# A gated FFN kernel: other order of SyncE's first loads, narrower first products of zeros, biases transposed behind q's product

## Chip, cores, metric

One Trainium2 chip, one core. The metric is the device time of one execution in microseconds (us). TensorE is called PE here, VectorE DVE, ScalarE ACT, GpSimd POOL, SyncE SP.

## What is computed

x has 128 batches of 32 rows of 256 (f32). With q = relu(cond · W3 + b3), one row of 256 for each batch, the reference does

```
c   = relu(((32 * x + sum of x over the 32 rows) * q) @ W2 + b2)
h1  = c @ w1q.T ;  h3 = c @ w3q.T          # hidden size 682
out = x + (silu(h1) * h3) @ w2q.T
wq  = clip(round(w / s), -1, 1) * s,  s = mean(|w|)   # for w1, w3, w2
```

## The kernel before, in words

The 4096 rows of x are eight groups of 512 rows, and each group is two halves of 256 rows. Half n goes through these steps: a product that brings it into transposed form, a scaling by q, a product with W2 (`project_c`), relu, and a split of the result into a high and a low part (`c_hi`, `c_lo`). A group then goes through six hidden steps (five blocks of 128 hidden units and a rest of 42): two products of four passes each, silu, product, split, and the output product. From about 21 us on, PE is nearly always busy with this loop.

The change is in the start, before that loop. Here the four engines run lists that are written out by hand, and semaphores tie them together:

- SP issues the loads in order: two bias loads of two rows each (`b_rows`, semaphore `got_b`), half 0 of x (`load_half(0)`), W2 (`got_W2`), halves 1 and 2 of x, then w1, w3, half 3, w2 and the other groups. ACT issues the loads of cond (`got_cond`) and W3 (`got_W3`) at the same time.
- DVE clears `blank`, a bf16 tile of zeros, then builds `mix`, the 128x128 matrix that both multiplies x by 32 and adds the sum over the sequence.
- PE multiplies zeros by zeros `WARM_UP` times (L422, nothing reads the results), transposes cond (L425), transposes the four bias rows into four columns (L427), does one more product of zeros (L428), and makes q's product in two chunks (L432, four recorded passes). ACT copies the transposed cond (L255) ahead of q's product, and DVE copies the bias columns (L605).
- ACT turns q's product into `qT` (L259). It needs the bias columns for that. DVE's first scaling waits for `qT`.
- `mix_x(n)` on PE (L377) is the transposing product of half n, eight recorded passes. DVE's `scale_mixed(n)` (L545) scales the result by q. `project_c(n)` (L391), eight recorded passes, needs the scaled half and W2. ACT's relu (L269) follows.
- ACT sums |w1| and |w3| (L278), PE adds these sums over the partitions (`sum_partitions`, L397), DVE makes a limit from each (L575) and compares the weights with it (L581). The compared weights are transposed on PE (L403) and their signs are taken on ACT (L284, L288). The first hidden products (L461) need them.

PE's order in the start is: products of zeros, cond, biases, zeros, q, `mix_x(0)`, `mix_x(1)`, `project_c(0)`, `mix_x(2)`, `project_c(1)`, `sum_partitions(0)`, `project_c(2)`, `sum_partitions(1)`, and then transposed weights and `mix_x(3)`.

Of the kernel before, what the change touches and what calls it, by code (L numbers as in the profile page):

```python
# [7 lines left out]
BF16 = mybir.dt.bfloat16  # L8
# [2 lines left out]
AX = mybir.AxisListType  # L11

P = 128
WARM_UP = 5
BANK = 512


def adaln_ternary_ffn_kernel(nc, x, cond, W3, b3, W2, b2, w1, w3, w2, out):
# [3 lines left out]
    DC = D // P  # L22
# [24 lines left out]
    with ExitStack() as ctx:  # L47
        def sb(name, shape, dt):
            return ctx.enter_context(nc.sbuf_tensor(name, shape, dt))

        def sem(name):
            return ctx.enter_context(nc.semaphore(name))

        cond_sb = sb("cond_sb", [P, Q], F32)
        b_rows = sb("b_rows", [2 * DC, P], F32)
# [22 lines left out]
        ident = sb("ident", [P, P], F32)  # L78
# [1 line left out]
        ones = sb("ones", [P, P], F32)  # L80

        mix = sb("mix", [P, P], F32)
        blank = sb("blank", [P, BANK], BF16)
        warm = sb("warm", [P, 1], F32)

        xo = sb("xo", [P, NG, TT, D], F32)
# [15 lines left out]
        bank = ctx.enter_context(nc.psum_tensor("bank", [P, 8, BANK], F32))  # L102
# [8 lines left out]
        b_cols_ps = bank[:, 3, 0:2 * DC]  # L111
# [13 lines left out]
        got_cond, got_W3, got_W2, got_b = sem("got_cond"), sem("got_W3"), sem("got_W2"), sem("got_b")  # L125
# [8 lines left out]
        b_cols_done, b_cols_copied = sem("b_cols_done"), sem("b_cols_copied")  # L134
# [39 lines left out]
        @block.sync  # L174
        def _(sp):
            for free in o_free:
                sp.sem_inc(free, 1)
            def load_half(n):
                g, h = n // HALVES, n % HALVES
                sp.dma_start(xo[:, g, h * HTT:(h + 1) * HTT], x_v[g, :, h * HTT:(h + 1) * HTT]).then_inc(got_half[n], 16)  # L180

            sp.dma_start(b_rows[0:DC, :], b3.rearrange("(c p) -> c p", p=P)).then_inc(got_b, 16)
            sp.dma_start(b_rows[DC:2 * DC, :], b2.rearrange("(c p) -> c p", p=P)).then_inc(got_b, 16)
            load_half(0)
            sp.dma_start(W2_sb[:], W2.rearrange("(c p) n -> p c n", p=P)).then_inc(got_W2, 16)
            load_half(1)
            load_half(2)

            sp.wait_ge(zeroed, 2)
            sp.dma_start(w1_sb[:, 0:HC, :], w1[0:HC * P, :].rearrange("(j p) d -> p j d", p=P)).then_inc(got_w1, 16)  # L190
            sp.dma_start(w1_sb[0:HR, HC, :], w1[HC * P:H, :]).then_inc(got_w1, 16)
            sp.dma_start(w3_sb[:, 0:HC, :], w3[0:HC * P, :].rearrange("(j p) d -> p j d", p=P)).then_inc(got_w3, 16)
            sp.dma_start(w3_sb[0:HR, HC, :], w3[HC * P:H, :]).then_inc(got_w3, 16)
            load_half(3)
            sp.dma_start(w2_sb[:], w2.rearrange("(c p) h -> p c h", p=P)).then_inc(got_w2, 16)
            for g in range(AHEAD, NG):
                if g == NG - 3:

                    sp.wait_ge(ternary_done, 5)
                sp.dma_start(xo[:, g], x_v[g]).then_inc(got_group[g - AHEAD], 16)  # L200
            for g in range(NG - 1):
                for b in range(TT // 2):
                    sp.wait_ge(o_free[b], g + 2)
                    sp.dma_start(out_v[g, :, 2 * b:2 * b + 2], xo[:, g, 2 * b:2 * b + 2]).then_inc(stored, 16)
            for b, t0, t1, n in ((0, 0, 2, 1), (1, 2, 3, 1), (1, 3, 4, 2)):
                sp.wait_ge(o_free[b], NG + n)
                sp.dma_start(out_v[NG - 1, :, t0:t1], xo[:, NG - 1, t0:t1]).then_inc(stored, 16)
            sp.wait_ge(stored, 16 * (NG * (TT // 2) + 1))
# [141 lines left out]
        def _(pe):  # L350
# [18 lines left out]
            def mix_x(n):  # L369

                pe.wait_ge(got_half[n], 16)
                bank_of_x_free(n)
                xT = xT_of(n)
                for c in range(DC):
                    for t in range(HTT):
                        col = c * HT + t * P
                        last = pe.matmul(xT[:, col:col + P],  # L377
                                         xo[:, n // HALVES, n % HALVES * HTT + t, c * P:(c + 1) * P], mix[:],
                                         start=True, stop=True)
                last.then_inc(xT_done, 1)  # L380
# [38 lines left out]

            pe.wait_ge(blank_ready, 1)  # L420
            for _ in range(WARM_UP):
                pe.matmul(bank[:, 7, :], blank[:, 0:P], blank[:], start=True, stop=True)  # L422
            pe.wait_ge(const_ready, 2)
            pe.wait_ge(got_cond, 16)
            pe.transpose(condT_ps, cond_sb[:], ident[:]).then_inc(condT_done, 1)  # L425
            pe.wait_ge(got_b, 16 * 2)
            pe.transpose(b_cols_ps, b_rows[:], ident[0:2 * DC, 0:2 * DC]).then_inc(b_cols_done, 1)  # L427
            pe.matmul(bank[:, 7, :], blank[:, 0:P], blank[:], start=True, stop=True)  # L428
            pe.wait_ge(got_W3, 16)
            pe.wait_ge(condT_copied, 1)  # L430
            for c in range(DC):
                pe.matmul(qT_ps[:, c, :], W3_sb[:, c * P:(c + 1) * P], condT[:], start=True, stop=True  # L432
                          ).then_inc(q_done, 1)
            pe.wait_ge(mix_ready, 6)
            mix_x(0)
            mix_x(1)
# [265 lines left out]
```

## Time and profile before

| | |
|---|---|
| median of 3 runs | 176.47 us (176.46 to 176.51) |
| profiled execution, its own time | 176.39 us |
| its span, first to last instruction | 174.2 us (so 2.2 us lie around it) |
| mean granted TensorE clock | 0.998 |
| PE busy | 169.4 us, 97% of the span |
| DVE, ACT, POOL busy | 59%, 50%, 20% |
| moved by DMA | 11.11 MB |

All times below are counted from the start of the span. In a row of the timeline the first number is the start, the second the time from the start of the first instruction to the end of the last of a merged group, and "x" the number of instructions in it. Passes of PE overlap, so a merged group tells more about the pace than the duration of one pass does. Brackets tell how long the engine was idle before and what ended that.

### The profile page before, as it was taken

The numbers are of one execution on the slowest core, as the hardware profiler recorded it, in microseconds if no ns is written. First come the engines' busy times: TensorE is split into PE (matmuls) and PEld (weight loads), VectorE is DVE, ScalarE is ACT, GpSimd is POOL, SyncE is SP. The second block draws the span as 40 slices with busy tenths as digits, with TensorE's granted clock in tenths as the row PEclk, the third lists the DMA queues.
The fourth block names the chain that finished last, engine by engine and source line by source line (L and its number), as shares of the span: only waits on it lengthen the run. The fifth ranks groups of instructions, "written<-read, shape, count | busy, mean of one in ns | idle before, by whom it ended". The sixth has DMA issues, their size and how long they took to land.

```text
span 174.2 us, 2563 instructions
## 1 busy us (share of the span) xinstructions
PE 169.4 (97%) x966; PEld 145.4 (83%) x966; DVE 103.1 (59%) x170; ACT 87.0 (50%) x161; POOL 34.6 (20%) x38
## 2 busy tenths in 40 slices
PE   7999999999999999999999999999999999999993
PEld 2988777888888888888889888888889888988792
DVE  2339939654864279353874369443874439456763
ACT  4169873645543372555534282554535285254640
POOL 5000005710505050320605041230605020000000
PEclk9999999999999999999999999999999999999999
DMA  4999082000030003000030003000030003000303
GB/s 141 311 360 349 32 268 93 0 4 4 0 120 0 4 0 120 0 0 4 0 120 0 0 4 109 11 0 0 4 120 0 0 4 120 4 0 0 120 4 120
DMA packets 10901, 11.11 MB, mean 64 GB/s; under 512 B 561, under 2 KB 10633, under 8 KB 10889
## 3 DMA queue, kind: packets, MB, share of 16 engines
q1 hardware_dynamic: 10600, 10.75, 18.8%
q10 hardware_dynamic: 288, 0.20, 0.4%
q8 instruction: 8, 0.13, 0.3%
q14 instruction: 5, 0.03, 0.1%
HBM read 6.75 MB, written 4.19 MB: 63 GB/s over the span
## 4 chain that ended last, share of the span: by engine, by line
PE 90%; DVE 3%; DMA 2%; SPq 1%; ACT 1%; POOL 1%; issue 0%; POOLq 0%; ACTq 0%
PE bank L461 46%; PE bank L490 24%; PE bank L391 15%; PE bank L365 3%; DMA xo<-in_x_dram 2%; DVE w_t L581 2%; PE bank L377 1%; POOL x L228 1%; PE bank L415 0%; DVE x L545 0%; DVE vsum L550 0%; DVE y L557 0%; ACT silu L323 0%; ACT T L284 0%; DVE xo L648 0%
## 5 line engine op out<-in xcount | busy, mean ns | idle before, releaser
L461 PE MATMUL bank<-c_hi,T 128*128 128x512 f32 (+1 forms) x176 | 71.1, 404 | 0.2 <-ACT T L288 0.2
L461 PE MATMUL bank<-c_lo,T 128*128 128x512 f32 (+1 forms) x176 | 69.5, 395 | 0.0
L323 ACT ACTIVATE silu<-bank,checked 128x512 f32<-128x512 f32 (+1 forms) x48 | 33.0, 688 | 72.1 <-PE bank L461 72.1
L635 DVE TENSOR_TENSOR gf<-silu,bank 128x512 f32<-128x512 f32 (+1 forms) x48 | 32.9, 685 | 53.4 <-PE bank L461 44.7
L461 PEld LDWEIGHTS bank<-c_hi,T 128*128 128x128 f32 (+1 forms) x176 | 32.8, 186 | 6.8 <-ACT T L288 0.6
L461 PEld LDWEIGHTS bank<-c_lo,T 128*128 128x128 f32 (+1 forms) x176 | 32.8, 187 | 6.2
L490 PE MATMUL bank<-T,g_hi 128*128 128x256 f32 x160 | 34.1, 291 | 0.0
L233 POOL TENSOR_TENSOR c_lo<-ct,c_hi 128x512 fp32r<-128x512 f32 x12 | 17.6, 1470 | 82.1 <-ACT c_hi L274 82.1
L490 PE MATMUL bank<-T,g_lo 128*128 128x256 f32 x160 | 32.6, 281 | 0.0
L391 PE MATMUL bank<-x,W_sb 128*128 128x256 f32 x128 | 30.5, 381 | 0.5 <-POOL x L228 0.4
L642 DVE TENSOR_TENSOR g_lo<-gf,g_hi 128x512 fp32r<-128x512 f32 x40 | 29.0, 724 | 1.2 <-ACT g_hi L330 1.2
L490 PEld LDWEIGHTS bank<-T,g_hi 128*128 128x128 f32 x160 | 26.5, 188 | 2.0
L391 PEld LDWEIGHTS bank<-x,W_sb 128*128 128x128 f32 x128 | 23.5, 190 | 4.0 <-POOL x L228 0.6
L490 PEld LDWEIGHTS bank<-T,g_lo 128*128 128x128 f32 x160 | 24.9, 188 | 0.0
L330 ACT CAST g_hi<-gf 128x512 fp32r<-128x512 f32 x40 | 24.5, 611 | 0.0
L228 POOL TENSOR_TENSOR x<-y,qT 128x512 f32<-128x512 f32 x12 | 12.6, 1050 | 23.3 <-DVE y L557 23.3
L269 ACT ACTIVATE ct<-bank,b_cols 128x256 f32<-128x256 f32 x32 | 13.3, 471 | 3.8 <-PE bank L391 3.8
L648 DVE SCALAR_TENSOR_TENSOR xo<-bank,out_scale,xo 128x512 f32<-128x512 f32 (+1 forms) x17 | 11.4, 709 | 1.4 <-PE bank L490 1.3
L550 DVE TENSOR_REDUCE vsum<-bank 128x16 f32<-128x512 f32 x12 | 8.2, 681 | 2.9 <-PE bank L365 2.9
L557 DVE SCALAR_TENSOR_TENSOR y<-bank,vsum 128x512 f32<-128x512 f32 x12 | 8.2, 685 | 0.2
L274 ACT CAST c_hi<-ct 128x512 fp32r<-128x512 f32 x12 | 7.6, 631 | 0.0
L365 PE MATMUL bank<-ident,xo 128*128 128x128 f32 x48 | 7.2, 273 | 0.0
(61 smaller groups left out, 82.4 us busy)
## 6 DMA issues: line engine op xcount, KB each, us to landing
out_dram<-xo SPq DMA_DIRECT2D x15, 256.0 KB, 2.2
xo<-in_x_dram SPq DMA_DIRECT2D x6, 512.0 KB, 7.3
w_sb<-in_L_ffn_w_dram SPq DMA_DIRECT2D x2, 640.0 KB
xo<-in_x_dram SPq DMA_DIRECT2D x4, 256.0 KB, 4.8
w_sb<-in_L_ffn_w_dram SPq DMA_DIRECT2D x1, 682.0 KB, 8.0
W_sb<-in_L_cond_W_dram SPq DMA_DIRECT2D x1, 256.0 KB, 3.9
out_dram<-xo SPq DMA_DIRECT2D x2, 128.0 KB, 2.1
W_sb<-in_L_cond_W_dram ACTq DMA_DIRECT2D x1, 128.0 KB, 2.5
```

The source lines that it names most:

```text
L228: nc.gpsimd.tensor_tensor(by_batch(flat(x1[:, n % 2])), by_batch(flat(y[:, n % 2])), over_sequence(flat(qT[:, n])), ALU.mult).then_inc(x1_ ...
L233: nc.gpsimd.tensor_tensor(half_of(c_lo, n), ct[:, n % NCT], half_of(c_hi, n).bitcast(F32), ALU.subtract).then_inc(c_lo_done, 1)
L269: nc.scalar.activation(ct[:, n % NCT, c, :], z_of(n)[:, c, :], ACT.Relu, bias=b2_col[c]).then_inc(relu_done, 1)
L323: nc.scalar.activation(silu[r, m % 2, :], h1[j % 2][r], ACT.Silu, scale=checked[r, 0:1]).then_inc(silu_done, 1)
L330: nc.scalar.copy(hi, gf[rows_of(j), m % 3, :]).then_inc(g_hi_done, 1)
L365: last = pe.transpose(xT[:, col:col + P], xo[:, n // HALVES, n % HALVES * HTT + t, c * P:(c + 1) * P], ident[:])
L391: last = pe.matmul(z[:, c, :], W2_sb[:, k, c * P:(c + 1) * P], x1[:, n % 2, k, :], start=(k == 0), stop=(k == DC - 1))
L461: last = pe.matmul(dst[j % 2][0:w, :], T13[:, k, col:col + w], part[:, g, k, :], start=(i == 0), stop=(i == len(passes) - 1))
L490: last = pe.matmul(out_ps, part[0:rows, t * P:(t + 1) * P], T2[0:rows, j, :], start=(j == 0 and i == 0 and n == 0), stop=(j == HC), skip_g ...
L635: nc.vector.tensor_tensor(gf[r, m % 3, :], silu[r, m % 2, :], second, ALU.mult).then_inc(g_done, 1)
L642: nc.vector.tensor_tensor(lo, gf[rows_of(j), m % 3, :], hi.bitcast(F32), ALU.subtract).then_inc(g_lo_done, 1)
L648: nc.vector.scalar_tensor_tensor(out=xg, in0=out_ps, scalar=out_scale[:, 0:1], in1=xg, op0=ALU.mult, op1=ALU.add).then_inc(o_free[b], 1)
```

## The change

It changes four things. SP issues half 0 of x first, then the two bias loads, half 1 of x, W2, and half 2. `blank` is 128 columns wide and not 512. The first products of zeros are 16 of 128 columns and not 5 of 512, and the later single one of 512 columns becomes 4 of 128. PE transposes the biases behind q's product and not ahead of it.

```diff
-WARM_UP = 5
+WARM_UP = 16
...
-        blank = sb("blank", [P, BANK], BF16)
+        blank = sb("blank", [P, P], BF16)
...
+            load_half(0)
             sp.dma_start(b_rows[0:DC, :], b3.rearrange("(c p) -> c p", p=P)).then_inc(got_b, 16)
             sp.dma_start(b_rows[DC:2 * DC, :], b2.rearrange("(c p) -> c p", p=P)).then_inc(got_b, 16)
-            load_half(0)
+            load_half(1)
             sp.dma_start(W2_sb[:], W2.rearrange("(c p) n -> p c n", p=P)).then_inc(got_W2, 16)
-            load_half(1)
             load_half(2)
...
             for _ in range(WARM_UP):
-                pe.matmul(bank[:, 7, :], blank[:, 0:P], blank[:], start=True, stop=True)
+                pe.matmul(bank[:, 7, 0:P], blank[:], blank[:], start=True, stop=True)
             pe.wait_ge(const_ready, 2)
             pe.wait_ge(got_cond, 16)
             pe.transpose(condT_ps, cond_sb[:], ident[:]).then_inc(condT_done, 1)
-            pe.wait_ge(got_b, 16 * 2)
-            pe.transpose(b_cols_ps, b_rows[:], ident[0:2 * DC, 0:2 * DC]).then_inc(b_cols_done, 1)
-            pe.matmul(bank[:, 7, :], blank[:, 0:P], blank[:], start=True, stop=True)
+            for _ in range(WARM_UP // 4):
+                pe.matmul(bank[:, 7, 0:P], blank[:], blank[:], start=True, stop=True)
             pe.wait_ge(got_W3, 16)
             pe.wait_ge(condT_copied, 1)
             for c in range(DC):
                 pe.matmul(qT_ps[:, c, :], W3_sb[:, c * P:(c + 1) * P], condT[:], start=True, stop=True
                           ).then_inc(q_done, 1)
+            pe.wait_ge(got_b, 16 * 2)
+            pe.transpose(b_cols_ps, b_rows[:], ident[0:2 * DC, 0:2 * DC]).then_inc(b_cols_done, 1)
```

## Rows read from the trace of the kernel before

**Rows 1.** The page: shares of the chain that ended last, by engine.

```profile
PE 90%; DVE 3%; DMA 2%; SPq 1%; ACT 1%; POOL 1%; issue 0%; POOLq 0%; ACTq 0%
```

**Rows 2.** Chain that ended last, in order of time, first 22 us: start, us, what.

```profile
0.86 0.36 SPq L182
...
1.57 0.41 SPq L180
...
2.02 0.47 SPq L185
...
2.53 4.26 DMA xo<-in_x_dram
```

**Rows 3.** Timeline of PE's weight loads, 0 to 30 us and narrower stretches.

```profile
4.94 1.63 PEld L377 LDWEIGHTS bank<-mix,xo 128*128 128x128 f32 x8
6.83 0.97 PEld L377 LDWEIGHTS bank<-mix,xo 128*128 128x128 f32 x8 [0.26 <-DMA xo<-in_x_dram]
...
4.94 1.19 PEld L377 LDWEIGHTS bank<-mix,xo 128*128 128x128 f32 x5
...
4.94 0.55 PEld L377 LDWEIGHTS bank<-mix,xo 128*128 128x128 f32 x2
```

**Rows 4.** Timeline of DVE, 0 to 30 us.

```profile
0.86 0.27 DVE L595 MEMSET blank<- 128x256 uint32 x1 [0.86 <-PEq L690]
1.11 0.17 DVE L596 MEMSET mix<- 128x128 f32 x1
...
6.87 0.69 DVE L545 TENSOR_TENSOR x<-bank,qT 128x512 f32<-128x512 f32 x1 [2.76 <-PE bank L377]
...
14.65 0.15 DVE L575 TENSOR_SCALAR limits<-bank 128x1 f32<-128x1 f32 x1
```

**Rows 5.** Timeline of PE's products, 0 to 30 us.

```profile
1.19 2.31 PE L422 MATMUL bank<-blank 128*128 128x512 bf16 x5 [1.19 <-DVE blank L595]
3.30 0.42 PE L425 MATMUL bank<-ident,cond_sb 128*128 128x128 f32 x1
3.65 0.26 PE L427 MATMUL bank<-ident,b_rows 4*128 4x4 f32 x1
3.84 0.61 PE L428 MATMUL bank<-blank 128*128 128x512 bf16 x1
4.24 1.11 PE L432 MATMUL bank<-condT,W_sb 128*128 128x128 f32 x4
...
7.83 1.89 PE L391 MATMUL bank<-x,W_sb 128*128 128x256 f32 x8
...
14.23 0.31 PE L397 MATMUL bank<-abs_sums,ones 128*128 128x1 f32 x2
```

**Rows 6.** DMA issues, each from a stretch of its own: KB, us to landing.

```profile
cond_sb<-in_cond_dram ACTq DMA_DIRECT2D x1, 64.0 KB, 1.8
W_sb<-in_L_cond_W_dram ACTq DMA_DIRECT2D x1, 128.0 KB, 2.5
xo<-in_x_dram SPq DMA_DIRECT2D x1, 256.0 KB, 2.9
W_sb<-in_L_cond_W_dram SPq DMA_DIRECT2D x1, 256.0 KB, 3.9
```

**Rows 7.** Timeline of ACT, 0 to 30 us.

```profile
0.73 0.38 ACTq L249 DMA_DIRECT2D cond_sb<-in_cond_dram  x1
1.14 0.46 ACTq L250 DMA_DIRECT2D W_sb<-in_L_cond_W_dram  x1
...
3.75 0.27 ACT L255 COPY condT<-bank 128x128 f32<-128x128 f32 x1 [0.63 <-PE bank L425]
...
12.53 1.48 ACT L278 ACTIVATE xo<-w_sb 128x1536 f32<-128x1536 f32 x1 [0.47 <-DMA w_sb<-in_L_ffn_w_dram]
```

**Rows 8.** Windows: stretch, length, busy PE, granted clock, DMA share, GB/s.

```profile
1.50:2.50 1.00, 1.00 (x4) 1.00 0.35 96
...
3.50:6.50 3.00, 3.00 (x16) 1.00 0.98 295
```

## The prediction

> **What bounds the kernel now.** I read the page's chain first: 90% of what ended last lies on PE [rows 1]. The changed lines all run before 7 us, so the question is how much earlier PE's work behind them can start. I take the loop behind 21 us as a fixed block: what the start gains, the end gains.
>
> Then I read the chain in order of time. It runs SP's two bias issues, half 0, W2, and then the transfer of half 1, which is issued at 2.53 and lands at 2.53 + 4.26 = 6.79. `mix_x(1)` follows it [rows 2]. Read alone, this chain says that half 1, issued one or two places sooner, is worth all the time by which it lands sooner.
>
> The weight loads on PE say otherwise. PE had only been idle 0.26 us when half 1 landed [rows 3], and DVE's first scaling, which `project_c(0)` also needs, started at 6.87, when `mix_x(0)` was done, not when half 1 was there [rows 4]. So two paths arrive almost together: half 1's transfer, and PE's own path over cond, q and `mix_x(0)`. The second is the one that must move.
>
> That path runs slowly. The first two weight loads of `mix_x(0)` take 0.55 us and the first five 1.19, so a pass takes (1.19 - 0.55) / 3 = 0.213. All eight at that pace would be 1.19 + 3 x 0.213 = 1.83. They took 1.63, and the eight of `mix_x(1)` 0.97 [rows 3]. This is the pace of the 1.2 GHz level and then of 2.4 GHz, although the window rows print a granted clock of 1.00 over both [rows 8]; I go by the pace. A slow pass costs (1.83 - 0.97) / 8 = 0.11 more than a fast one, and 1.63 is 0.20 under 1.83, so the clock rose two passes before the end of `mix_x(0)`, at about 6.3.
>
> **The change, part by part.**
>
> *Smaller `blank`.* The clearing of 256 words takes 0.27, that of 128 words 0.17 [rows 4]. For 64 words I take 0.12 (bounds 0.09 and 0.17, so a gain of 0.10 to 0.18). PE starts at 1.19 - 0.15 = 1.04.
>
> *16 x 128 for 5 x 512.* One takes 0.61 by itself (the equal product at 3.84), so the five follow each other every (2.31 - 0.61) / 4 = 0.425 us [rows 5]. A quarter of the columns is 0.106, if each product's own weight load hides behind it (the slow f32 passes, with a load each, keep twice that, 0.213). Sixteen take 1.70, against 2.11 from 1.19 to 3.30. They end at 1.04 + 1.70 = 2.74. cond lands at 0.73 + 1.8 = 2.5 [rows 6, 7], so it is there, but barely. I put cond's transpose at 2.80, against 3.30: 0.50 earlier. ACT's copy then ends at 4.02 - 0.50 = 3.52.
>
> *4 x 128 for 1 x 512 and no biases in between.* After cond's transpose (0.35, from 3.30 to 3.65 [rows 5]) the four take 0.43, so PE has work until 2.80 + 0.35 + 0.43 = 3.58. The next work is q's product, and it needs W3.
>
> *W3.* It lands at 1.14 + 2.5 = 3.64 [rows 6, 7]. Until now that cost nothing. Now it is the late one. Half 0 is also issued 0.71 sooner, at 0.86, and its 256 KB flow beside W3's 128 KB on the same DMA engines. Lower bound of that cost: nothing, because the DMA engines were busy only 0.35 from 1.5 to 2.5 [rows 8]. Upper bound: W3 waits behind another 128 KB at 295 GB/s, 0.43. I take 0.1, near the lower bound, because of the idle share: 3.75. From the end of the copy (4.02) to q's first pass (4.24) is 0.22; from a landing, with the weight load still to do, I take 0.2. So q starts at 3.95 (bounds 3.84 and 4.27) against 4.24: 0.29 earlier.
> The Trainium skill, "DMA: Bandwidth & Descriptors", section "Queues, rings and completion order", says that each DMA engine takes turns between the queues it has work for. By it W3 would share with half 0 and never stand behind all of it, and q would start at about 3.95 too; no row shows the two at once.
>
> *Biases behind q.* They held PE for 3.84 - 3.65 = 0.19 [rows 5], and now hold it between q and `mix_x(0)`. They land behind half 0, before 4.5 (half 0 before: 1.57 + 2.9 [rows 2, 6]), and PE comes to them behind q's four passes, at 3.95 + 4 x 0.213 = 4.80. DVE's copy and ACT's `qT` follow before 6.0, under `mix_x(0)`. So the loads of `mix_x(0)` start at 4.84 against 4.94 [rows 3], only 0.10 earlier: of the 0.50 won in front of q, 0.21 go to W3 and 0.19 to the biases.
>
> *`mix_x(0)`.* If the clock rises at 6.3 as before, 0.10 more of slow time saves 0.10 x 0.97 / 1.83 = 0.05 at the end. DVE's scaling starts at 6.82 and ends at 7.51.
>
> *Half 1 before W2.* It takes the issue slot of W2, which was issued at 2.02 and landed after 3.9, at 5.9 [rows 2, 6]. So it lands at 5.9 or sooner, which is 0.9 earlier and no longer counts. W2 lands no later than half 1 did (6.8); it is needed at 7.7. SP's issues of w1, w3 and the rest keep their places.
>
> *Sum.* `project_c(0)` started at 7.83 behind `mix_x(1)`. Now `mix_x(1)` follows `mix_x(0)` at once and ends near 7.5, and PE waits for DVE's scaling at 7.51. From a copy's end to PE's first pass is 0.22, as above: 7.73. The gain is 7.83 - 7.73 = 0.10, with bounds of -0.03 (W3 at its latest) and 0.2 (W3 at its earliest, all of the 0.18 at `blank`). Against the profiled execution's own 176.39 that is 176.29; against the median of 176.47, which I forecast, it is about 176.37, and I say 176.35.
>
> **Rivals.**
>
> *A: as summed.* 176.35, range 176.15 to 176.5.
>
> *B: the clock rises earlier than 6.3.* The moment is known from one execution only. Before, an earlier rise was worth nothing, since half 1 landed at 6.79 whatever PE did, and so the equal times of three runs do not show when the clock rose. Now half 1 is early, and each us by which the rise comes sooner ends `mix_x(0)` 1 - 0.97 / 1.83 = 0.47 us sooner. At 0.5 us sooner the gain is 0.10 + 0.24 = 0.34. Then another bound comes: w3's transfer. ACT was idle 0.47 for it until 12.53 [rows 7], and the sum made from it left PE at 14.23 + 0.31 = 14.54, only 0.11 before DVE took it for its limit at 14.65 [rows 4, 5]. So the slack there is 0.1. The whole stream of loads starts 0.71 sooner; I take half of that, 0.35, for w3's landing (bounds 0 and 0.71, since cond and W3 use part of the time won). The gain is capped at 0.45 (0.1 to 0.8): 176.0.
> The Trainium skill, "TensorE: Matmul & The Clock Gate", section "What you observe", says that the rise varies by 500 ns from run to run. By it some executions would gain 0.34 and some nothing; the rows of one execution neither bear it out nor speak against it.
>
> *C: W3 leaves a hole and the clock rises later (the other side).* PE was never idle from 1.19 to 6.5. Now it has nothing from 3.58 to 3.95, and longer if W3 is late. If the rise is put off for that, `mix_x(1)` and `project_c(0)` run at half pace: up to 0.9 + 1.7 us more. It decides once the rise comes about 0.9 later (0.9 x 0.47 = 0.42, against a gain of 0.10 and the 0.35 that can be told). A rise in the middle of `project_c(0)` gives about 177.5. Against it: the hole is short beside 5 us of work.
>
> *D: the chain as it stands is right.* Half 1's 0.9 would count in full, 175.6. Against it stands the idle time of 0.26; it could only come together with B, and w3 caps it. I count it under B.
>
> **How the numbers follow.** A measurement of this kernel can tell about 0.2%, 0.35 us, from no change. A 0.52, B 0.36, C 0.12. A lies within 0.35, so "same" is 0.52; B is "faster" but for its mildest part, which A's largest gains make up for, 0.36; C "slower", 0.12. The range leaves C and B's far end (0.07) out: 175.85 to 176.6. A's own range is given above.
>
> **What the profile after would show.** Zeros starting at 1.04 and about 0.107 apart; cond's transpose near 2.80; q's first pass near 3.95 with the wait in front of it put down to W3; the biases 0.2 behind it; `mix_x(0)`'s first load at 4.84; no wait for half 1; DVE's first scaling at 6.82 and `project_c(0)` at 7.73. B would show fewer slow passes in `mix_x(0)` and a scaling well before 6.8, and then ACT's wait for w3 grown. C would show passes of 0.214 behind 7 us. The prediction is wrong if W3 lands much later than 3.8, or if the pace changes elsewhere.

## The result, and the profile after

The changed kernel is slower. Its median is 177.82 us (177.04 to 178.49, 6 runs) against 176.47 us (175.76 to 176.58, 6 runs) before. The ratio is 1.0082, 95% interval [1.0052, 1.0113]. Ratios leave out executions more than 1.5% above the fastest of their kernel; medians and ranges do not. The spread is as new as the median: 1.45 us against 0.82. The profiled execution took 177.04 us, the fastest of the six, with a span of 174.9 against 174.2. So the trace below shows 0.65 of a loss (177.04 against 176.39), where the medians differ by 1.35.

The timeline of PE's products, changed kernel:

```profile
0.99 1.89 PE L422 MATMUL bank<-blank 128*128 128x128 bf16 x16 [0.99 <-DVE blank L596]
3.14 0.45 PE L425 MATMUL bank<-ident,cond_sb 128*128 128x128 f32 x1 [0.27 <-DMA cond_sb<-in_cond_dram]
3.38 0.63 PE L427 MATMUL bank<-blank 128*128 128x128 bf16 x4
4.08 1.22 PE L431 MATMUL bank<-condT,W_sb 128*128 128x128 f32 x4
5.23 0.26 PE L434 MATMUL bank<-ident,b_rows 4*128 4x4 f32 x1
5.42 3.26 PE L377 MATMUL bank<-mix,xo 128*128 128x128 f32 x16
8.52 1.89 PE L391 MATMUL bank<-x,W_sb 128*128 128x256 f32 x8
```

The zeros begin and end sooner than in [rows 5], as planned. But PE then stands idle for cond. q's product begins at 4.08, only 0.16 sooner than the 4.24 of before, and `project_c(0)` at 8.52, 0.69 later than 7.83. The span grew by 0.7, so all of the loss in this execution lies ahead of 8.52, and the loop behind it only moved.

That holds in all twenty profiled executions of this document: from the first weight load of `sum_partitions(0)` (12.17 before, 12.86 after) to the end of the span it is 162.0 to 162.2. Every difference between their spans, 173.7 to 176.6, is made in the first 11.7 to 14.5 us.

The timeline of its weight loads, against [rows 3]:

```profile
4.08 0.93 PEld L431 LDWEIGHTS bank<-condT,W_sb 128*128 128x128 f32 x4 [0.33 <-DMA W_sb<-in_L_cond_W_dram]
5.23 0.18 PEld L434 LDWEIGHTS bank<-ident,b_rows 4*128 4x128 f32 x1 [0.22 <-issue]
5.42 3.07 PEld L377 LDWEIGHTS bank<-mix,xo 128*128 128x128 f32 x16
8.41 1.59 PEld L391 LDWEIGHTS bank<-x,W_sb 128*128 128x128 f32 x8
```

The third row is the one to read. The sixteen loads of `mix_x(0)` and `mix_x(1)` take 3.07. All at the slow pace would be 15 x 0.213 + 0.33 = 3.53, all at the fast one 15 x 0.11 + 0.19 = 1.84 (0.33 and 0.19 are what a single slow and a single fast load take; below, s2_first has all sixteen slow in 3.49 and s3_two all fast in 1.86). A slow one costs 0.107 more, so 3.07 holds about four fast ones: PE was at its 1.2 GHz level until 5.42 + 12 x 0.213 = 8.0. Before, that was 6.3. There is no wait for half 1 any more.

The chain that ended last, in order of time, now runs over W3 and PE where [rows 2] had half 1:

```profile
1.14 2.90 DMA W_sb<-in_L_cond_W_dram
...
4.08 1.22 PE bank L431 x4
5.30 0.20 PE bank L434
5.49 3.19 PE bank L377 x16
8.68 1.73 PE bank L391 x8
```

DMA issues, each from a stretch of its own (KB, us to landing), against [rows 6]:

```profile
cond_sb<-in_cond_dram ACTq DMA_DIRECT2D x1, 64.0 KB, 2.3
W_sb<-in_L_cond_W_dram ACTq DMA_DIRECT2D x1, 128.0 KB, 2.9
xo<-in_x_dram SPq DMA_DIRECT2D x1, 256.0 KB, 4.1
```

cond and W3 are issued at the same moments as before and land 0.5 and 0.4 later, at 3.0 and 4.0. Of the 0.4 a part is chance. In the ten profiled executions in which the biases come before half 0, W3 took 2.2 (e9_both) to 2.9 (e5_hole), in the ten with half 0 in front 2.9 to 3.4. For cond the two sets do not meet: 1.8 to 2.0 and 2.2 to 2.8. Half 1, issued at 2.04, lands at 6.1.

### The profile page after: what moved, and what is told of

It reads as the page before. It is cut to its first block, busy times and chain, and to the rows that moved or that the text cites. A ratio compares the mean times of both kernels' runs of the same rounds, so it can differ in the third digit from the quotient of the medians.

```text
span 174.9 us, 2591 instructions
## 1 busy us (share of the span) xinstructions
PE 170.0 (97%) x980; PEld 147.3 (84%) x980; DVE 102.9 (59%) x170; ACT 87.1 (50%) x161; POOL 34.7 (20%) x38
## 4 chain that ended last, share of the span: by engine, by line
PE 91%; DVE 3%; DMA 2%; ACT 1%; POOL 1%; issue 0%; ACTq 0%; POOLq 0%
PE bank L462 46%; PE bank L491 24%; PE bank L391 15%; PE bank L365 3%; PE bank L377 2%; DVE w_t L582 2%; DMA W_sb<-in_L_cond_W_dram 2%; PE bank L431 1%; POOL x L228 1%; PE bank L415 0%; DVE y L558 0%; DVE vsum L551 0%; ACT silu L323 0%; DVE x L546 0%; ACT T L284 0%
## 5 line engine op out<-in xcount | busy, mean ns | idle before, releaser
L365 PEld LDWEIGHTS bank<-ident,xo 128*128 128x128 f32 x48 | 5.9, 140 | 1.6
```

Source lines behind the costliest of these rows:

```text
L365: last = pe.transpose(xT[:, col:col + P], xo[:, n // HALVES, n % HALVES * HTT + t, c * P:(c + 1) * P], ident[:])
```

## The experiments

There were eighteen runs, in five groups; the kernels of a group shared a chip. Four of them run a kernel for the second time: e11_again the changed one, s2_first e8_first, s3_two e4_filled, and t2_ahead e9_both. The last columns give what the text uses most: how many executions took over 177.2 us (of the kernel before: 7 of 162, over all groups), and how long the sixteen loads of `mix_x(0)` and `mix_x(1)` took in the profiled execution. "+ wait" marks those that held a wait for half 1.

| run | what differs | median (range), us | ratio, 95% interval | over 177.2 | 16 loads, us |
|---|---|---|---|---|---|
| changed | | 177.82 (177.04 to 178.49) | 1.0082 [1.0052, 1.0113] | 5 of 6 | 3.07 |
| e1_wide | changed, wide zeros | 176.75 (176.34 to 178.44) | 1.0029 [1.0002, 1.0055] | 5 of 12 | 1.86 |
| e2_narrow | before, narrow zeros | 176.39 (176.01 to 176.79) | 0.9989 [0.9976, 1.0001] | 0 of 12 | 1.54, 0.97 + wait |
| e3_order | before, new order of loads | 176.90 (176.59 to 177.68) | 1.0024 [1.0008, 1.0040] | 4 of 12 | 2.56 |
| e4_filled | changed, 20 and 6 zeros | 176.88 (175.84 to 178.12) | 1.0015 [0.9994, 1.0037] | 2 of 12 | 1.96 |
| e5_hole | before, 2 wide zeros, none later | 177.28 (176.34 to 179.41) | 1.0040 [1.0019, 1.0060] | 7 of 12 | 3.14 |
| e6_half1 | e2_narrow, half 1 before W2 | 176.61 (175.53 to 177.65) | 1.0010 [0.9988, 1.0031] | 2 of 12 | 2.21 |
| e7_biases | before, biases behind q | 176.59 (175.89 to 178.19) | 1.0024 [0.9995, 1.0052] | 3 of 12 | 0.97, 0.97 + wait |
| e8_first | changed, 20 and 4 zeros | 177.90 (175.88 to 178.74) | 1.0062 [1.0033, 1.0091] | 10 of 12 | 3.49 |
| e9_both | e6_half1, 18 and 6 zeros | 176.46 (176.01 to 176.82) | 0.9979 [0.9958, 1.0000] | 0 of 12 | 1.86 |
| e10_dense | changed, 22 and 6 zeros | 176.61 (175.96 to 178.39) | 1.0018 [0.9989, 1.0047] | 3 of 12 | 2.50 |
| e11_again | changed, same chip as e10 | 177.45 (177.28 to 178.54) | 1.0057 [1.0034, 1.0080] | 9 of 9 | 2.96 |
| e12_old_order | e2_narrow, 18 and 6 zeros | 176.29 (175.94 to 176.67) | 0.9986 [0.9970, 1.0002] | 0 of 12 | 0.98, 0.97 + wait |
| s1_second | changed, 16 and 6 zeros | 177.41 (177.08 to 177.96) | 1.0053 [1.0036, 1.0070] | 7 of 8 | 2.81 |
| s2_first | changed, 20 and 4 zeros | 177.75 (175.85 to 178.41) | 1.0042 [1.0007, 1.0077] | 7 of 12 | 3.49 |
| s3_two | changed, 20 and 6 zeros | 176.98 (176.16 to 178.13) | 1.0033 [1.0009, 1.0057] | 5 of 12 | 1.86 |
| s4_pe_only | changed, SP's order as before | 176.89 (176.44 to 211.72) | 1.0025 [1.0007, 1.0043] | 5 of 12 | 3.49 |
| t1_behind | e9_both, biases behind q | 176.30 (175.65 to 178.03) | 0.9997 [0.9966, 1.0027] | 2 of 12 | 1.86 |
| t2_ahead | e9_both again | 176.38 (175.85 to 177.38) | 0.9997 [0.9972, 1.0022] | 2 of 12 | 2.66 |

One execution of s4_pe_only took 211.72 us; I do not read it.

### One part at a time

e1_wide undoes the narrow zeros, e2_narrow does them alone, e3_order does SP's order alone, and e7_biases, of the next group, moves the biases alone. The expectations weigh three theories. Narrow products: zeros of 128 columns keep PE slow for longer. Holes: stretches in which PE has nothing to do, in front of cond's transpose or of q, put off its fast pace. Load order: the late landings are the cost by themselves.

```diff
 # e1_wide, against the changed kernel
-WARM_UP = 16
+WARM_UP = 5
...
-                pe.matmul(bank[:, 7, 0:P], blank[:], blank[:], start=True, stop=True)
+                pe.matmul(bank[:, 7, :], blank[:, 0:P], blank[:], start=True, stop=True)
...
-            for _ in range(WARM_UP // 4):
+            for _ in range(1):
```

Expected of e1_wide:

> The changed kernel with the products of zeros as they were before (5 and 1 of 512 columns); SP's order and the moved biases stay. Narrow-products theory (products of 128 columns keep the slow pace longer): the rise comes before 6.5 us again and the time is 176.47 or up to 0.4 under it (176.1 to 176.5). Hole theory (PE runs dry at 2.87 while cond is late): the five wide products last until 3.3, past cond's landing at about 3.0, so the hole in front of cond is gone, and the time is also 176.1 to 176.6. Load-order theory (W3's landing, now 0.4 us later, and biases ahead of mix_x(0) are the cost by themselves): still slower, 176.9 to 177.8.

Expected of e2_narrow (all of the change's edits to the zeros, on the kernel before):

> The kernel before with only the products of zeros narrowed (16 and 4 of 128 columns, small blank tile); SP's order and the biases as before. Narrow-products theory: as slow as the changed kernel, 177.4 to 178.2, with slow passes beyond 7.5 us. Hole theory: cond lands at 2.6, before the zeros end at 2.7, so there is no hole in front of it, and only a short one ahead of W3: 176.3 to 176.8. Load-order theory: same as before, 176.3 to 176.6.

Expected of e3_order (the edit to SP's list alone):

> The kernel before with only SP's order of loads changed. Narrow-products theory and hole theory: no slower than before, 176.0 to 176.6, since the wide products cover cond's landing at about 3.0. Load-order theory: cond and W3 land 0.4 us later, and the biases behind half 0 hold up PE in front of q: 176.9 to 177.8.

Expected of e7_biases:

> The kernel before with only the transpose of the biases moved behind q's product. Worked out from its trace: q is held by the copy of cond (4.02) and not by PE, so its start stays at 4.24 or comes 0.1 sooner, and mix_x(0) starts 0.1 to 0.2 later: 176.5 to 176.7, no more than 0.1 over before. Hole theory: without the biases between cond and the wide product nothing runs dry for more than 0.1 us; same.

Narrow zeros are not to blame by themselves: with them alone the kernel is at 176.39 with no execution over 177.2. That ends the narrow-products theory. But wide zeros took back much of the changed kernel's loss: e1_wide is at 1.0029. They last until 3.5, so that in its profiled execution cond's transpose followed them without a wait, and all sixteen loads of `mix_x` were fast. Its 176.75 lies in none of the ranges expected of it, and 5 of 12 executions took over 177.2 with no hole in the trace. What these are comes at the end of "Which hole". The other two parts cost something each, but less than the whole: SP's order 0.24%, and the biases' place raised 3 of 12 executions over 177.2, with an interval that still holds no change. The timeline of PE's products in e3_order shows what the order alone does:

```profile
3.29 0.42 PE L425 MATMUL bank<-ident,cond_sb 128*128 128x128 f32 x1
4.10 0.26 PE L427 MATMUL bank<-ident,b_rows 4*128 4x4 f32 x1 [0.38 <-DMA b_rows<-in_L_cond_b_dram]
```

The biases, now behind half 0 in SP's queue, hold PE until 4.10, where [rows 5] had 3.65: the order alone makes a hole too, of 0.38. My expectation for this run had looked at cond alone, and its 176.0 to 176.6 for the hole theory was too low for that.

### Holes in front of cond and q

The next question was whether a PE that stands idle before q is the cause. e5_hole makes such holes in the kernel before, with its own order of loads; e4_filled, e8_first and e10_dense fill the holes of the changed kernel by more zeros; e11_again is the changed kernel beside e10_dense.

```diff
 # e5_hole, against the kernel before
-WARM_UP = 5
+WARM_UP = 2
...
-            pe.matmul(bank[:, 7, :], blank[:, 0:P], blank[:], start=True, stop=True)
 # e4_filled, against the changed kernel
-WARM_UP = 16
+WARM_UP = 20
...
-            for _ in range(WARM_UP // 4):
+            for _ in range(6):
```

> The changed kernel with more narrow products: 20 in place of 16 and 6 in place of 4, so that PE has work until cond and W3 have landed (about 3.1 and 4.1 us). Hole theory: the rise comes back to about 6.3 and the time to 176.1 to 176.7. Narrow-products theory: stays slow, 177.3 to 178.3, with slow passes beyond 7.5 us though PE is never idle. Load-order theory: 177.0 to 178.

> The kernel before, SP's order untouched, with only 2 products of zeros of 512 columns and none behind the biases, so that PE runs dry from about 2.0 to 2.9 us and again before q, while every load lands as before. Hole theory (a PE that runs dry before q gets the fast clock later): slow passes through mix_x(1) and project_c(0), 177.2 to 178.6, though q itself starts up to 0.4 us sooner. Load-order theory (late cond and W3 are the cost by themselves): 176.2 to 176.7.

> The changed kernel with 20 in place of 16 narrow products in front of cond and still 4 behind it. This closes the hole in front of cond (0.3 to 0.5 us) and leaves the one in front of q (about 0.3). Hole theory: between the changed kernel (177.8) and the one with both holes filled (176.9), 177.0 to 177.6 if both holes count by their length; near 176.9 if only the first matters. Load-order theory: 177.8 as the changed kernel.

> The changed kernel with 22 and 6 narrow products. Hole theory: the holes in front of cond and q are closed in most executions, 176.4 to 176.9, about 1 us under the changed kernel on the same chip. Load-order theory: half 0 in front delays cond and W3 by 0.4 us whatever PE does, 177.3 or more.

> The changed kernel, unchanged, for a second profile and as the measure on this chip. Hole theory: 177.6 to 178.2 with the slow passes lasting until 7.5 us or later. If its slowness were a matter of the first chip or of chance, 176.5 to 177.

e5_hole is the cleanest of these. PE's timeline and its weight loads, where only the products of zeros are fewer:

```profile
1.19 1.03 PE L422 MATMUL bank<-blank 128*128 128x512 bf16 x2 [1.19 <-DVE blank L594]
2.74 0.45 PE L425 MATMUL bank<-ident,cond_sb 128*128 128x128 f32 x1 [0.52 <-DMA cond_sb<-in_cond_dram]
...
4.09 1.22 PE L431 MATMUL bank<-condT,W_sb 128*128 128x128 f32 x4 [0.70 <-DMA W_sb<-in_L_cond_W_dram]
```

```profile
4.89 3.14 PEld L377 LDWEIGHTS bank<-mix,xo 128*128 128x128 f32 x16
```

The work of PE begins no later than before: q at 4.09 against 4.24, the first load of `mix_x(0)` at 4.89 against 4.94. Yet the slow pace lasts through most of `mix_x(1)`, and 7 of 12 executions take over 177.2, against 2 of 35 of the kernel before on the same chip. So work that does nothing but keep PE busy was worth 0.4% here, and taking it away is enough for a loss. (This profiled execution is one of the five under 177.2, at 176.56, and W3 took 2.9 in it and not 2.5, which made the second hole longer than planned.)

With both holes filled the changed kernel comes back to 176.61 in e10_dense, beside 177.45 for the changed kernel on the same chip: 0.84 us, though half 0 still goes first. That ends the load-order theory in its plain form, in which the late landings are the cost by themselves. e4_filled, at 176.88, is just above the 176.1 to 176.7 that the hole theory gave it. Filling only the first hole did nothing in e8_first: 177.90, outside the 176.9 to 177.6 of the hole theory and just what the load-order theory said. Its profiled execution, at 178.74 the longest of the twelve, had the hole after all: cond landed so late that PE was idle for it 0.38 us, until 3.68, and the loads were slow to the end.

### Which hole

Four kernels on one chip try to tell the holes apart.

> The changed kernel with 16 narrow products in front of cond and 6 in place of 4 behind it: the hole in front of q is filled, the one in front of cond stays. If the second hole is the one that counts: 176.6 to 177.0. If the first one: 177.6 to 178. If their sum: about 177.3.

> The changed kernel with 20 and 4: the hole in front of cond is filled when cond lands by 3.1 us, the one in front of q stays. If the second hole is the one that counts: 177.5 to 178 again. If the first one, or their sum: under 177.4.

> The changed kernel with 20 and 6: both holes filled. All forms of the hole theory: 176.5 to 177.0, the lowest of the three.

> The changed kernel with SP's order of loads as before: PE's part of the change alone. Hole theory: cond lands at 2.6 and leaves no hole of more than 0.2 us in front of its transpose, W3 at 3.6 to 3.9 leaves one of up to 0.2 in front of q: 176.4 to 177.0. If PE's part alone is enough for the loss (narrow products with biases behind q): 177.5 or more.

The weight loads of s2_first (20 and 4 zeros):

```profile
4.29 0.93 PEld L431 LDWEIGHTS bank<-condT,W_sb 128*128 128x128 f32 x4 [0.32 <-DMA W_sb<-in_L_cond_W_dram]
5.44 0.18 PEld L434 LDWEIGHTS bank<-ident,b_rows 4*128 4x128 f32 x1 [0.23 <-issue]
5.64 3.49 PEld L377 LDWEIGHTS bank<-mix,xo 128*128 128x128 f32 x16
```

and of s3_two (20 and 6):

```profile
4.32 0.71 PEld L431 LDWEIGHTS bank<-condT,W_sb 128*128 128x128 f32 x4
5.15 0.13 PEld L434 LDWEIGHTS bank<-ident,b_rows 4*128 4x128 f32 x1
5.30 1.86 PEld L377 LDWEIGHTS bank<-mix,xo 128*128 128x128 f32 x16
```

The two differ by two products of zeros, 0.2 us of work. In the first, PE's loads stand idle 0.32 us for W3 and all sixteen loads are slow; in the second they do not wait in front of q, and q's own loads are already partly fast. By themselves the two traces prove little, since one kernel can differ nearly as much from itself: the sixteen loads took 1.86 in e9_both and 2.66 in t2_ahead, with a rise before 4.8 and at 6.5. And the times of s2_first fall into two groups, five executions at 175.85 to 176.24 and seven at 177.62 to 178.41. A hole makes the late rise frequent; it does not force it. s1_second has the other hole. Its timelines of products and of weight loads:

```profile
3.34 0.45 PE L425 MATMUL bank<-ident,cond_sb 128*128 128x128 f32 x1 [0.46 <-DMA cond_sb<-in_cond_dram]
```

```profile
5.63 2.81 PEld L377 LDWEIGHTS bank<-mix,xo 128*128 128x128 f32 x16
```

Neither hole alone is the cause. Over 177.2 were 7 of 8 executions with the first hole open, 17 of 24 with the second (e8_first, s2_first), 15 of 48 with neither (e1_wide, e4_filled, e10_dense, s3_two), and 14 of 15 of the changed kernel with both. This rests on all groups together. On the one chip the medians are in the same order (177.41, 177.75, 176.98), but 7 of 12 in s2_first against 5 of 12 in s3_two tells nothing apart, and neither do their ratios.

The profiled executions agree, with a narrow overlap. Worked out as for the changed kernel, the rise came at 6.8 or later in the seven in which PE's products stood idle 0.27 us or more in front of cond, the biases or q (changed, e3_order, e5_hole, e8_first, e11_again, s1_second, s4_pe_only), and beyond 9.1 in s2_first, where the loads were idle and the products hardly. In the twelve others it came at 6.9 or sooner. s4_pe_only had cond at its old time and still had 5 of 12 over 177.2; its q waited 0.38 us for W3 because q could have begun sooner than W3 landed. So SP's order is not needed for a part of the loss.

The rest that s3_two keeps over the kernel before (176.53 in that group) is not explained by a hole. Weight loads of `sum_partitions(0)` in e4_filled and in s3_two, two executions of one kernel, both with an early rise:

```profile
11.69 0.30 PEld L397 LDWEIGHTS bank<-abs_sums,ones 128*128 128x128 f32 x2 [0.24 <-issue]
```

```profile
12.95 0.30 PEld L397 LDWEIGHTS bank<-abs_sums,ones 128*128 128x128 f32 x2 [1.34 <-issue]
```

The loads stood idle 1.34 in s3_two because ACT got w1 only at 11.26 (after 1.01 of waiting), where e4_filled began its sum of |w1| at 10.01 without a wait. That 1.26 is all of the difference between 177.26 and 175.84 but 0.2. e1_wide shows the same, with 1.20 idle. So a late w1 is a second way to a long execution, and it needs no hole.

t1_behind and t2_ahead asked whether it is the biases' place.

> As the run with both (biases loaded first, half 1 before W2, 18 and 6 narrow products), with the biases transposed behind q instead of ahead. If the gap that this leaves between q and mix_x(0) (about 0.2 us idle and a product of 4 columns) also puts off the clock: 2 to 6 of 12 executions over 177.2 us, median 176.6 to 177. If only the holes in front of cond and q count: none over 177.2, median 176.4 to 176.6.

> The run with both again, biases ahead of q, beside it on the same chip: 176.3 to 176.5, none or one over 177.2 us, ratio to the kernel before 0.997 to 1.000.

It is not shown: 2 of 12 in each, medians 176.30 and 176.38. t2_ahead is also the same kernel as e9_both, which had 0 of 12, so two executions of twelve are within chance. The theory is not borne out, and twelve executions each can't rule out a small effect.

### A better version

e6_half1, e9_both and e12_old_order keep the biases in front and look for what is left of the idea.

```diff
 # e6_half1 and e9_both, against e2_narrow
-            sp.dma_start(W2_sb[:], W2.rearrange("(c p) n -> p c n", p=P)).then_inc(got_W2, 16)
             load_half(1)
+            sp.dma_start(W2_sb[:], W2.rearrange("(c p) n -> p c n", p=P)).then_inc(got_W2, 16)
 # e9_both and e12_old_order, against e2_narrow
-WARM_UP = 16
+WARM_UP = 18
...
-            for _ in range(WARM_UP // 4):
+            for _ in range(6):
```

> Narrow products of zeros as in the run with them alone, biases first and transposed ahead of q as before, and half 1 issued before W2. cond and W3 are not held up by half 0, so PE runs dry only shortly. Hole theory: the rise stays where it was with the narrow products alone, PE no longer waits 0.33 us for half 1, and the time is 0.2 to 0.5 under that run's 176.39: 175.9 to 176.3. Load-order theory (what costs is half 0 ahead of everything else): also 175.9 to 176.3. If an early half 1 by itself makes the time sensitive to the rise, it spreads over more than 1 us.

> Biases loaded and transposed first as before, half 1 issued before W2, 18 narrow products of zeros in front of cond and 6 behind the biases, so that PE has work until about 4.1 us. Hole theory: the rise never comes later than before, an early rise now pays because half 1 is there, and the time is under the kernel before: 175.8 to 176.3, with no run over 177.2. If the spread of the run with half 1 early (175.5 to 177.7) has another cause than holes, the median stays at 176.5 to 176.7.

> SP's order as before, biases ahead of q, 18 narrow products of zeros in front of cond and 6 behind the biases. It is the run with both, without half 1 before W2. Hole theory: as the kernel before or 0.1 to 0.2 under it, 176.3 to 176.5, because half 1 holds PE whenever the clock rises early. So the run with both should lie 0.2 to 0.4 under this one.

e9_both reached 0.9979 [0.9958, 1.0000], and 0.9997 [0.9972, 1.0022] when it ran again as t2_ahead. e12_old_order reached 0.9986 [0.9970, 1.0002]. None is shown to beat the kernel before by 0.2%. And half 1 before W2 brought nothing over e12_old_order (176.46 against 176.29), where 0.2 to 0.4 was expected; e6_half1 (176.61, expected 175.9 to 176.3) and e9_both (expected 175.8 to 176.3) missed their ranges too. ACT's timeline in e9_both suggests why:

```profile
8.91 0.84 ACT L269 ACTIVATE ct<-bank,b_cols 128x256 f32<-128x256 f32 x2 [3.45 <-PE bank L391]
10.62 1.48 ACT L278 ACTIVATE xo<-w_sb 128x1536 f32<-128x1536 f32 x1 [0.87 <-DMA w_sb<-in_L_ffn_w_dram]
12.01 0.19 ACT L278 ACTIVATION_READ_ACCUMULATOR xo<-w_sb 128x1 f32 x1
12.74 1.49 ACT L278 ACTIVATE xo<-w_sb 128x1536 f32<-128x1536 f32 x1 [0.55 <-DMA w_sb<-in_L_ffn_w_dram]
```

and the same of e12_old_order:

```profile
9.45 0.84 ACT L269 ACTIVATE ct<-bank,b_cols 128x256 f32<-128x256 f32 x2 [3.65 <-PE bank L391]
10.18 1.48 ACT L278 ACTIVATE xo<-w_sb 128x1536 f32<-128x1536 f32 x1
11.55 0.20 ACT L278 ACTIVATION_READ_ACCUMULATOR xo<-w_sb 128x1 f32 x1
11.64 1.48 ACT L278 ACTIVATE xo<-w_sb 128x1536 f32<-128x1536 f32 x1
```

relu came 0.54 sooner in e9_both, but w1 was not there: ACT waited 0.87 us, and began the sum of |w1| 0.44 later. The chain of e9_both has `4.06 6.53 DMA` of w1 in the place of half 1. In this execution the next transfer took back what PE had gained in front. It need not: in t2_ahead, the same kernel, ACT found w1 there at 10.42, but PE's rise was late (6.5). How often each of the two decides is not known.

## Why the prediction was wrong, by its own steps

**The failed step** is rival C's dismissal: "Against it: the hole is short beside 5 us of work." The mechanism was named and priced (177.5), with a chance of 0.12. In the profiled execution PE's products stood idle 0.27 us for cond and its weight loads 0.33 for W3, in that of e11_again 0.55 and 0.30, and the fast pace came at 8.0 in both (5.67 + 11 x 0.213 = 8.0 for e11_again), where it had come at 6.3. A long time is the usual course, not the rare one: 14 of 15 executions took over 177.2. e5_hole, which only takes products of zeros out of the kernel before, shows that the holes are enough for a loss (1.0040), and e10_dense, which fills them, that most of it goes with them (1.0018 beside 1.0057 on the same chip).

**`blank` and the zeros.** Right. They began at 0.99 (forecast 1.04); the sixteen loads took 1.62, a pace of 0.1.

**cond.** "So it is there, but barely": it was not. It landed at 3.0 and not 2.5, because half 0 flowed beside it (in s4_pe_only, with SP's old order, it took 1.8 again). The transpose was at 3.14, not 2.80. The prediction asked what an early half 0 costs W3, and did not ask it for cond, which stands in front of W3 in ACT's queue.

**W3.** Mis-sized. The term was 0.1 with bounds of 0 and 0.43; measured 0.4, next to the upper bound. But the 2.5 that it started from was one execution's, and with the biases in front of half 0 W3 took anything from 2.2 to 2.9; a term read from one landing needed that width. I chose the lower end by the idle share of the DMA engines. The Trainium skill, "DMA: Bandwidth & Descriptors", section "Queues, rings and completion order", says that an engine takes turns between its queues; the landings of both cond and W3 behind an early half 0 agree with sharing, though that did not make it cheap. q was at 4.08 (forecast 3.95).

**Biases behind q.** Mis-sized. From q's first load to the first of `mix_x(0)` the kernel before took 4.94 - 4.13 = 0.81 (4.13 is the start of q's loads in its timeline), the changed one 5.42 - 4.08 = 1.34. That is 0.53, not 0.19. Besides the product itself, the row shows loads idle for 0.22 in front of the biases. I read it as the wait there stopping the loads that otherwise run ahead of the products; no run takes out the wait alone. e7_biases shows the same, 5.41 - 4.13 = 1.28.

**`mix_x(0)` and the sum.** Its loads began at 5.42 (forecast 4.84). Had the fast pace come at 6.3 all the same, 0.48 more of slow work would have cost about 0.48 x 0.97 / 1.83 = 0.25. `project_c(0)` was 0.69 later. The other 0.44, by this reckoning, is the later rise of the pace. That is the profiled execution; the median's loss of 1.35 needs still later rises, or late loads, in the others. s2_first and e8_first show rises beyond 9.1, with spans of 176.0 and 176.6. That the loop behind only moves was right: 0.69 there, 0.7 in the span. The sum's lower bound was off as well: with W3 at its latest q starts 0.32 later, which is 0.10 - 0.32 x 0.97 / 1.83 = -0.07 and not -0.03. It would not have changed the forecast.

**Half 1.** Right in that its wait went away; it landed at 6.1, near the 5.9 forecast.

**Rival B** was half right. An early rise does come (e4_filled, s3_two, e9_both), and one execution of e6_half1 took 175.53. The five executions of s2_first at 175.85 to 176.24 are 0.3 to 0.7 under the kernel before, which is the size that B forecast; that their rise was early is argued, since none of them was profiled. But the 0.35 by which w3 was to land sooner can't be seen: with the new order ACT waited for it until 12.02 in e4_filled and until 13.39 in s3_two, on both sides of the 12.53 of [rows 7]. The Trainium skill, "TensorE: Matmul & The Clock Gate", section "What you observe", gives the rise a scatter of 500 ns from run to run; here it came before 4.8 in e9_both and at 6.5 in t2_ahead, one kernel, and beyond 9.1 in s2_first, so the measurement decides for much more.

**What stays open.** Each run has one profiled execution, so that the executions over 177.2 are mostly those with a late rise is argued, not shown for each. Six of the profiled ones took over 177.2: e8_first, e11_again, s1_second, s2_first and s4_pe_only with a late rise, and s3_two with an early one and a late w1. How the 15 of 48 executions with both holes filled divide between the two, and whether half 0 in front makes w1 late more often, is not settled. Nor is it known why a hole of 0.3 us moves the rise by more than its own length.

## What to carry to other kernels

Products of zeros in front of the real work are not mere filling: size them to the latest landing they must cover, with a margin, and not to the time that they take from the real work. A load that is moved to the front of one queue can be paid for by what flows at that moment on another: cond, issued 0.13 us ahead of half 0, still landed 0.5 later. Where several paths arrive together, as half 1, PE and w1 did here, a shorter one may bring nothing until the others follow. And a moment read from one execution (the rise at 6.3, W3's 2.5) is a draw from a range: look at more than one before a sum leans on tenths.

## What the runs showed of the hardware

Taking products of zeros out of the kernel before made it 0.4% slower (e5_hole, 1.0040). The rise of PE's pace scattered by more than 1.7 us between two executions of one kernel (before 4.8 in e9_both, 6.5 in t2_ahead). The granted clock of the window rows read 1.00 in slow and fast stretches alike (5.50 to 6.50 and 8.50 to 10.00 in the changed kernel), so that only the pace of equal instructions told the level. The landings of w1 and w3 scattered by over 1 us between executions of one kernel: ACT waited for w1 until 11.26 in s3_two and found it there at 10.01 in e4_filled, and waited for w3 until 13.39 and 12.02. cond took 1.8 to 2.0 us to land with half 0 behind the biases and 2.2 to 2.8 with half 0 in front, though it was issued first. And a wait of PE for a tiny transpose behind q went with 0.5 us in place of 0.19 between q's loads and the next (1.28 in e7_biases against 0.81), 0.2 of it with the weight loads idle.
